# A gated cross-attention block with a mixture of experts: moving the low halves of expert weights to GpSimd and the shared chunk's first products into the last scores

## The chip, the cores and the metric

The kernel runs on one core of a Trainium2 chip. The metric is device microseconds of one execution. The core's engines are TensorE (PE, with its weight loads as PEld), VectorE (DVE), ScalarE (ACT), GpSimd (POOL) and SyncE (SP, which here only issues DMAs). Each engine has its own queue of instructions and works it off in order; semaphores order the engines against each other.

## What is computed

```python
def block(x, ctx, mask, g_xattn, g_ffn, ...):          # x: 16 x 128 x 256
    x = x + tanh(g_xattn) * cross_attention(layernorm(x), ctx, mask)   # 16 heads of 16
    h = layernorm(x)                                    # 2048 tokens of 256
    top2, idx = top_k(h @ w_router, 2)                  # 8 experts
    moe = sum over the 2 chosen e: softmax(top2)[e] * ((silu(h @ fc1[e][:, :256]) * (h @ fc1[e][:, 256:])) @ fc2[e])
    shared = (silu(h @ gate_w) * (h @ up_w)) @ down_w   # inner width 512
    return x + tanh(g_ffn) * (moe + shared)
```

## The kernel before, in words

The 2048 tokens are worked in G = 8 groups of 256 for the attention, and in 4 chunks of 512 for the shared feed-forward part. The attention of group g runs in a software pipeline over steps s: keys, queries, scores (once for the row maxima, once transposed for the exponentials), values, the second normalization, the router, and the places of the tokens in the experts' lists. All engines' orders are written out by hand, function by function.

**The way to the experts.** When the attention of the last group (g = 7) ends, four things have to be done before the first expert tile can start:

- The routing of the last units. `logits`, `choice` and `chosen` (DVE) make one-hot choices, `positions` (PE, lines 1527 to 1548) counts them, `places` (DVE, from line 1048) turns them into row numbers, `weights` (DVE, from line 1068) writes the weight and the destination into the rows and raises `w_ok`. Then `dispatch(g)` (POOL, lines 529 to 543) scatters the group's rows with four indirect DMAs into the DRAM tensor `dispatched`. `dispatch(7)` waits for `w_ok` of the last unit.
- `table` (DVE, lines 1186 to 1215) makes three things: `pads_ok`, on which SP issues eight DMAs of zero rows (line 451); `table_ok`, the row number of every tile; `words_ok`, the expert of every tile, which PE reads into registers (lines 1720 to 1723). SP loads the first tiles (line 473) when all scatters and pads have landed.
- The weights are split into a high half (ACT, `high_of_fc1` line 704, `high_of_fc2` line 778) and a low half, weight minus high half (`low_of_fc1`, line 1174, `low_of_fc2`, line 1180, both on DVE in the kernel before). There are E = 8 experts; one fc1 half is 128 x 1024 numbers, one fc2 half 128 x 512. PE waits for all 8 fc1 low halves ahead of the first `expert_h` (line 1771) and for all fc2 low halves ahead of the first `expert_y` (line 1797). GpSimd makes the low halves of the shared gate, up and down weights at line 589, after `f2lo_ok` has reached 8.
- The shared part of chunk 0 (`shared_0` line 1550, then `down_0` line 1582) and of chunk 1 (`shared_1(n)`, line 1567, n = 0 to 15, four to a block j of 128 hidden columns; then the loop at line 1730, in which `expert_x` transposes the first two tiles). ACT's `gate_silu` (line 787) and DVE's `times` (line 1168) take a block each from PSUM. `sum_and_add` (line 1158) adds the chunk's result.

From there 39 expert tiles follow each other on PE (lines 1810 to 1823). For each, GpSimd scatters the result (line 597); DVE's `expert_dst` (line 1269) writes the number of tile n into one of four places and waits until the scatter of tile n - 4, which used the place before, has landed. Chunks 2 and 3 of the shared part end the kernel.

PSUM banks of chunk 1: `BANKS_1` gives block j the banks (gate, up) by j % 2; the score tiles use banks 0 and 1, the transposed ones 2 and 3.

Of the kernel before, what the change touches and what calls it, by code (L numbers as in the profile page):

```python
# [7 lines left out]
ALU = mybir.AluOpType  # L8
ACT = mybir.ActivationFunctionType
F32 = mybir.dt.float32  # L10
# [43 lines left out]
def build_program(nc, x, ctx_t, mask, gates, wq, wk, wv, w_router, fc1, fc2, gate_w, up_w, down_w, out):  # L54
# [23 lines left out]
    with ExitStack() as es:  # L78
# [245 lines left out]

        BANKS_0 = (5, 6)
        EARLY = 4
        BANKS_1 = [(2, 3), (0, 1)]

        def live(g):

# [161 lines left out]
        def _(pool):  # L492
# [36 lines left out]
            def dispatch(g):  # L529
                u = g // 2 if g < 6 else g - 3  # L530
                if g == units[u][0]:
                    pool.wait_ge(slots_ok, u + 1)
                    pool.wait_ge(w_ok, u + 1)
                    pool.wait_ge(dup_ok[0], units[u][-1] + 1)
                    pool.wait_ge(dup_ok[1], units[u][-1] + 1)
                for m in range(4):
                    if (g, m) == (G - 4, 1):
                        power2(G - 1, 0)
                    if (g, m) == (G - 3, 0):
                        power2(G - 1, 1)  # L540
                    nc.gpsimd.indirect_dma_start(  # L541
                        xs, bass.IndirectOffsetOnAxis(slot_u[:, g, m:m + 1], 0), rows_of[g][:, m, :], None,
                        bounds_check=NULL_ROW + P - 1, oob_is_err=False).then_inc(scat[u == 1] if g else scat_first, 16)
# [27 lines left out]
            for s in range(2, G + 2):  # L571
# [6 lines left out]
                if live(s):  # L578
                    third(s, kst, k_rest, k_ok[1], k_pc, k_ok[2])
                    stack_k_high(s)  # L580
                    third(s, qst, q_rest, q_ok[1], q_pc, q_ok[2])

            dispatch(G - 4)
            dispatch(G - 3)
            dispatch(G - 2)
            dispatch(G - 1)

            def low_half(low, w, high):
# [16 lines left out]
                    low_half(xt_lo[:, :, tokens], xt_all[:, :, tokens], xt_hi[:, 2 * c - 4:2 * c - 2, :])  # L605


            for n, (low, w, high) in enumerate(((gate_lo, gate_s, gate_hi), (up_lo, up_s, up_hi),
                                                (down_lo, down_s, down_hi))):
                pool.wait_ge(gu_done, NJ)  # L610
                pool.wait_ge(f2lo_ok, E)
                if n == 2:
                    pool.wait_ge(down_done, 2 * CH)
                pool.wait_ge(high_ok, n + 1)
                low_half(low[:, :, :], w[:, :, :], high[:, :, :])
# [5 lines left out]
        def _(sa):  # L621
# [156 lines left out]
            def high_of_fc2(e):  # L778

                if e < EARLY:  # L780
                    sa.wait_ge(fc2_in, 16 * EARLY)
                else:
                    sa.wait_ge(fc2_late, 16 * (E - EARLY))
                nc.scalar.activation(fc2_hi[:, 2 * e:2 * e + 2, :], fc2_s[:, 2 * e:2 * e + 2, :],
                                     ACT.Copy).then_inc(f2hi_ok, 1)

            def gate_silu(c, j, bank):
                sa.wait_ge(gu_done, (c - 1) * NJ + j + 1)
                if c == 1 and j < 2:
                    sa.wait_ge(scat[1], ALL_1)  # L790
                else:
                    sa.wait_ge(hid_ok, (c - 1) * NJ + j - 1)
                nc.scalar.activation(sil_sh[:, j % 2], ps[:, bank, :], ACT.Silu).then_inc(sil_ok, 1)
# [36 lines left out]
            gate_silu(1, 1, BANKS_1[1][0])  # L830
            for e in range(6, E):
                high_of_fc1(e)
            for e in range(E):
                high_of_fc2(e)
            sa.wait_ge(scat_first, 64)
            sa.wait_ge(scat[0], ALL_0)
            sa.wait_ge(scat[1], ALL_1)
            sa.wait_ge(down_done, CH)
            high_half(gate_hi[:, :, :], gate_s[:, :, :])
            gate_silu(1, 2, BANKS_1[0][0])  # L840
            high_half(up_hi[:, :, :], up_s[:, :, :])
            gate_silu(1, 3, BANKS_1[1][0])
            high_half(down_hi[:, :, :], down_s[:, :, :])

            def rows_in_halves(t, d):
# [57 lines left out]
        def _(ve):  # L903
# [273 lines left out]
                nc.vector.tensor_tensor(fc1_lo[:, 2 * e:2 * e + 2, :], fc1_s[:, 2 * e:2 * e + 2, :],  # L1177
                                        fc1_hi[:, 2 * e:2 * e + 2, :].bitcast(F32), ALU.subtract).then_inc(flo_ok, 1)

            def low_of_fc2(e):  # L1180

                ve.wait_ge(f2hi_ok, e + 1)
                nc.vector.tensor_tensor(fc2_lo[:, 2 * e:2 * e + 2, :], fc2_s[:, 2 * e:2 * e + 2, :],  # L1183
                                        fc2_hi[:, 2 * e:2 * e + 2, :].bitcast(F32), ALU.subtract).then_inc(f2lo_ok, 1)

            def table():

                ve.wait_ge(pos_done, len(units))
# [48 lines left out]
            logits(g)  # L1237
            choice(g)
            chosen(g)
            places(g)  # L1240
            weights(g)
            table()
            relink()
            times(1, 0)
            times(1, 1)
            for e in range(3):
                low_of_fc1(e)
            sum_and_add(0, 0, sums_0)
            for e in range(3, 7):
                low_of_fc1(e)  # L1250
            times(1, 2)
            low_of_fc1(7)
            for e in range(3):
                low_of_fc2(e)
            times(1, 3)
            for e in range(3, E):
                low_of_fc2(e)

            def expert_rows(t, d):

# [102 lines left out]
        def _(pe):  # L1363
# [203 lines left out]
            def shared_1(n):  # L1567

                j, up, k = n // 4, n // 2 % 2, n % 2
                if n == 0:  # L1570
                    pe.wait_ge(xt_ok, 4)
                    pe.wait_ge(probs_ok[1][1], G)
                elif n == 4:
                    pe.wait_ge(max_ok[1][1], G)
                elif n % 4 == 0:
                    pe.wait_ge(hid_ok, j - 1)
                last = nc.tensor.matmul(ps[:, BANKS_1[j % 2][up], :], (gate_s, up_s)[up][:, k, P * j:P * j + P],
                                        xt_all[:, k, CH * P:2 * CH * P], start=k == 0, stop=k == 1)
                if n % 4 == 3:
                    last.then_inc(gu_done, 1)  # L1580
# [39 lines left out]
            for s in range(2, G + 2):  # L1620
                if live(s - 1):
                    queries(s - 1)
                if live(s - 2):
                    scores(s - 2, 1, 0)
                    if s == G + 1:
                        shared_0(6)
                    max_t(s - 2, 0)
                if live(s - 3):
                    values(s - 3, 1, 0)
                    values(s - 3, 1, 1)  # L1630
                if s == G + 1:
                    shared_0(7)
                if live(s - 4):
                    router(s - 4)
                if live(s - 2):
                    scores(s - 2, 1, 1)
                if live(s):
                    normed_t(s)
                    keys_main(s)
                if live(s - 3):  # L1640
                    values_t(s - 3, 1)
                if live(s - 2):
                    scores_t(s - 2, 0, 0)
                    if s == G:
                        shared_0(0)
                        shared_0(1)
                    if s == G + 1:
                        shared_0(8)
                if live(s):
                    values_main(s)  # L1650
                if live(s - 2):
                    max_t(s - 2, 1)
                if live(s):
                    for c in range(2):
                        keys_rest(s, c)
                        values_rest(s, c)
                if s == G:
                    shared_0(2)
                    shared_0(3)
                if s == G + 1:  # L1660
                    shared_0(9)
                    shared_0(10)
                if live(s - 2):
                    scores_t(s - 2, 0, 1)
                if live(s - 1):
                    scores(s - 1, 0, 0)
                if live(s - 4):
                    positions(s - 4)
                if live(s - 2):
                    values(s - 2, 0, 0)  # L1670
                    values(s - 2, 0, 1)
                    if s == G + 1:
                        shared_0(11)
                    scores_t(s - 2, 1, 0)
                if live(s - 1):
                    scores(s - 1, 0, 1)
                if s == G:
                    shared_0(4)
                if live(s - 2):
                    values_t(s - 2, 0)  # L1680
                if live(s - 3):
                    tokens_t(s - 3)
                if s == G:
                    shared_0(5)
                if live(s - 2):
                    scores_t(s - 2, 1, 1)

            g = G - 1
            values(g, 1, 0)
            router(g - 1)  # L1690
            values(g, 1, 1)
            values_t(g, 1)
            for n in range(12, 16):
                shared_0(n)
            positions(g - 1)
            tokens_t(g)
            shared_1(0)
            shared_1(1)
            router(g)
            for n in range(2, 5):  # L1700
                shared_1(n)
            positions(g)
            for n in range(5, 8):
                shared_1(n)
            for t in range(CH):
                down_0(t)
            for n in range(8, 16):
                shared_1(n)
# [175 lines left out]
```

## Time and profile before

| | |
|---|---|
| median of 3 runs | 333.09 us (332.68 to 334.06) |
| span of the profiled execution, first to last instruction | 329.2 us |
| the profiled execution's own time | not given apart; the runs' median lies 3.9 us above the span |
| PE, DVE, ACT, POOL busy | 304.6, 243.6, 169.2, 129.8 us |
| mean granted TensorE clock | 0.983 of full speed |
| first expert product | starts 190.84 us into the span |

Line numbers (L1177) are lines of the kernel. In a timeline a row gives the start, the duration, the engine, the line, the operation with output and inputs, how many instructions are merged (x4), and in brackets how long the engine was idle before and who ended that. In the chain of waits a row is one piece of the chain that ended last, with its start and its length.

### The profile page before, as it was taken

What the parts mean: (1) busy time and instruction counts of PE and PEld (TensorE: products, weight loads), DVE (VectorE), ACT (ScalarE), POOL (GpSimd) and SP (SyncE); (2) the same over time, 40 slices, a digit from 0 to 9 for tenths busy, and PEclk for the clock granted to TensorE, in tenths of its full rate; (3) what the DMA queues carried; (4) which work ended last, traced back from release to release, by engine and by line L of the source; (5) the groups of instructions that cost most, each with busy time, mean ns of one, the idle gap of its engine ahead of it and who ended that gap; (6) DMA issues with size and microseconds to landing.
All of it is one profiled execution on the core that took longest, in us unless ns stands there. A gap on an engine that the chain in (4) does not pass through costs nothing.

```text
span 329.2 us, 8082 instructions
## 1 busy us (share of the span) xinstructions
PE 304.6 (93%) x2505; PEld 244.5 (74%) x2505; DVE 243.6 (74%) x728; ACT 169.2 (51%) x322; POOL 129.8 (39%) x151
## 2 busy tenths in 40 slices
PE   7948889999989979998999989999999999999986
PEld 7627667787768755655465758889988898888875
DVE  4576597798999998687679976666666666633895
ACT  2444767777777744365495236444454444424131
POOL 5732143232465744506760085744333433331000
PEclk9998999999999999996999999999999999999999
DMA  7882776586666362166226112333333333103941
GB/s 232 255 217 80 227 197 207 161 263 193 189 186 177 123 178 84 50 201 250 98 98 164 44 34 83 106 94 108 94 103 98 97 85 111 64 16 133 416 153 64
DMA packets 34069, 47.18 MB, mean 143 GB/s; under 512 B 5519, under 2 KB 27667, under 8 KB 33522
## 3 DMA queue, kind: packets, MB, share of 16 engines
q1 hardware_dynamic: 28706, 34.61, 35.3%
q0 software_dynamic: 4320, 10.92, 9.9%
q10 hardware_dynamic: 1008, 1.18, 1.2%
q8 instruction: 22, 0.36, 0.5%
q14 instruction: 13, 0.11, 0.1%
HBM read 22.20 MB, written 12.62 MB: 106 GB/s over the span
## 4 chain that ended last, share of the span: by engine, by line
PE 41%; DVE 18%; issue 17%; POOL 8%; DMA 7%; SPq 5%; ACT 2%; POOLq 0%; DVEq 0%
PE ps L1744 27%; POOL dispatched L541 4%; DMA stacks<-work 4%; DVE x_all L1334 3%; DVE fc_lo L1177 3%; SPq L381 3%; PE ps L1790 3%; PE ps L1716 2%; PE ps L1562 2%; POOL rs L526 2%; PE ps L1437 1%; SPq L374 1%; DVE fc_lo L1183 1%; DMA stacks<-expert_rows 1%; PE ps L1407 1%
## 5 line engine op out<-in xcount | busy, mean ns | idle before, releaser
L597 POOL DMA_INDIRECT expert_rows<-v_s,slot_u x39 | 38.3, 982 | 58.6 <-ACT v_s L867 46.3
L963 DVE TENSOR_REDUCE mx<-ps 128x8 f32<-128x1024 f32 x32 | 39.1, 1223 | 13.0 <-PE ps L1437 12.7
L1284 DVE TENSOR_TENSOR act<-ps,sil 128x256 f32<-128x256 f32 x39 | 16.6, 425 | 29.9 <-ACT sil L860 29.8
L549 POOL TENSOR_TENSOR work<-work 128x512 bf16<-128x512 f32 x16 | 18.5, 1156 | 50.3 <-ACT work L646 50.2
L677 ACT ACTIVATE probs<-ps 128x1024 f32<-128x1024 f32 x32 | 32.7, 1022 | 9.4 <-PE ps L1470 9.4
L860 ACT ACTIVATE sil<-ps 128x256 f32<-128x256 f32 x39 | 15.0, 384 | 41.4 <-PE ps L1744 41.3
L1744 PE MATMUL ps<-fc_hi,xs_hi 128*128 x78 | 34.2, 439 | 1.4 <-DVE xs_lo L1265 1.4
L1744 PE MATMUL ps<-fc_hi,xs_lo 128*128 x78 | 30.7, 394 | 0.0
L1744 PE MATMUL ps<-fc_lo,xs_hi 128*128 x78 | 30.7, 394 | 0.0
L867 ACT ACTIVATE v_s<-ps,wt 128x256 f32<-128x256 f32 x39 | 18.5, 475 | 19.0 <-PE ps L1744 19.0
L1437 PE MATMUL ps<-stacks 96*128 96x128 bf16 x256 | 20.1, 222 | 7.0 <-DVE mx L963 3.3
L1437 PEld LDWEIGHTS ps<-stacks 96*128 96x128 bf16 x256 | 16.0, 100 | 10.3 <-DVE mx L963 4.8
L1744 PE MATMUL ps<-fc_hi,act_hi 128*128 x78 | 22.1, 283 | 0.2 <-DVE act_lo L1295 0.2
L1744 PE MATMUL ps<-fc_lo,act_hi 128*128 x78 | 22.0, 282 | 0.0
L1744 PE MATMUL ps<-fc_hi,act_lo 128*128 x78 | 21.9, 281 | 0.0
L1470 PEld LDWEIGHTS ps<-stacks 99*128 99x128 bf16 x256 | 15.8, 98 | 6.9 <-issue 5.4
L1470 PE MATMUL ps<-stacks 99*128 99x128 bf16 x256 | 19.7, 220 | 0.5 <-ACT probs L677 0.5
L1486 PE MATMUL ps<-probs,v_s 128*32 128x128 f32 x512 | 18.6, 281 | 1.1 <-DVE att L985 0.8
L1293 DVE CAST act_hi<-ps 128x256 fp32r<-128x256 f32 x39 | 16.5, 423 | 3.2 <-PE ps L1790 3.2
L541 POOL DMA_INDIRECT dispatched<-row_s,slot_u x16 | 16.0, 1000 | 7.4 <-issue 4.1
L1295 DVE TENSOR_TENSOR act_lo<-ps,act_hi 128x256 fp32r<-128x256 f32 x39 | 16.6, 424 | 1.3
L526 POOL TENSOR_TENSOR rs<-ve,mhalf 128x1 f32<-128x1 f32 x16 | 9.1, 566 | 21.4 <-DVE ve L996 21.4
(221 smaller groups left out, 828.4 us busy)
## 6 DMA issues: line engine op xcount, KB each, us to landing
stacks<-work SPq DMA_DIRECT2D x75, 128.0 KB, 3.1
xs_in<-dispatched SPq DMA_DIRECT2D x39, 129.0 KB, 2.0
fc_s<-in_fc SPq DMA_DIRECT2D x8, 512.0 KB, 5.2
stacks<-work POOLq DMA_DIRECT2D x18, 128.0 KB, 3.4
ctx_s<-in_ctx_t SPq DMA_DIRECT2D x8, 256.0 KB, 3.7
fc_s<-in_fc SPq DMA_DIRECT2D x8, 256.0 KB, 5.3
stacks<-expert_rows SPq DMA_DIRECT2D x2, 1024.0 KB, 5.8
probs<-expert_rows SPq DMA_DIRECT2D x2, 1024.0 KB, 9.9
```

The lines of the kernel that those rows point to most:

```text
L541: nc.gpsimd.indirect_dma_start(xs, bass.IndirectOffsetOnAxis(slot_u[:, g, m:m + 1], 0), rows_of[g][:, m, :], None, bounds_check=NULL_ROW + ...
L549: nc.gpsimd.tensor_tensor(out[:, 2, :], rest, out[:, 1, :], ALU.subtract).then_inc(ready, 1)
L597: nc.gpsimd.indirect_dma_start(ys, bass.IndirectOffsetOnAxis(dst_u[:, r:r + 1], 0), y_out[:, r, :], None, bounds_check=2 * T - 1, oob_is_e ...
L677: nc.scalar.activation(probs[:, 2 * j + h], ps_t, ACT.Exp, scale=HD ** -0.5).then_inc(probs_ok[j][h], 1)
L867: nc.scalar.activation(y_out[:, r, :], ps[:, 5 + r % 2, 0:D], ACT.Copy, scale=wt[:, r:r + 1]).then_inc(y_ok, 1)
L963: nc.vector.reduce_max(mx[:, j, 8 * h:8 * h + 8], ps_s, AX_X).then_inc(max_ok[j][h], 1)
L1284: nc.vector.tensor_tensor(act[:, par], ps[:, 2 + par, FI:2 * FI], sil[:, par], ALU.mult).then_inc(act_ok, 1)
L1295: nc.vector.tensor_tensor(act_lo[:, par], whole, act_hi[:, par].bitcast(F32), ALU.subtract).then_inc(actt_ok, 1)
L1437: last = nc.tensor.matmul(ps_s[:, n, :], q_st[at], k_st[at], start=True, stop=True)
L1470: last = nc.tensor.matmul(ps_t[:, n, :], k_st[at], q_st[at], start=True, stop=True)
L1486: last = nc.tensor.matmul(ps_o[row:row + VW, blk:blk + P], v_s[:, g % 2, j, VW * head:VW * head + VW], probs[:, 2 * j + h, n, :], start=Tr ...
L1744: ins = nc.tensor.matmul(out, a, b, start=first and n == 0, stop=last and n == 2)
```

## The change

The low halves of fc2 (8) and those of fc1's experts 0 and 1 move from DVE to GpSimd. The two fc1 ones stand between `dispatch(6)` and `dispatch(7)`, the eight fc2 ones behind `dispatch(7)` and ahead of the shared weights' low halves. On PE the first four `shared_1` calls move into the end of group 7's attention, `shared_1(4)` to `(7)` ahead of the last router, and `down_0(0)` ahead of the last `positions`. `BANKS_1` is swapped, and with it which wait stands at n = 0 and n = 4. On DVE one fc1 low half goes between `chosen(7)` and `places(7)`, the two first `times(1, j)` go around `weights(7)` and ahead of `table`, and the other low halves are put between the sums and products. On ACT `gate_silu(1, 2)` and `(1, 3)` go ahead of the wait for the scatters.

```diff
-        BANKS_1 = [(2, 3), (0, 1)]
+        BANKS_1 = [(0, 1), (2, 3)]
...
+            def low_of_fc1(e):
+                pool.wait_ge(fhi_ok, e + 1)
+                nc.gpsimd.tensor_tensor(fc1_lo[:, 2 * e:2 * e + 2, :], fc1_s[:, 2 * e:2 * e + 2, :],
+                                        fc1_hi[:, 2 * e:2 * e + 2, :].bitcast(F32), ALU.subtract).then_inc(flo_ok, 1)
+
+            def low_of_fc2(e):
+                pool.wait_ge(f2hi_ok, e + 1)
+                nc.gpsimd.tensor_tensor(fc2_lo[:, 2 * e:2 * e + 2, :], fc2_s[:, 2 * e:2 * e + 2, :],
+                                        fc2_hi[:, 2 * e:2 * e + 2, :].bitcast(F32), ALU.subtract).then_inc(f2lo_ok, 1)
...
             dispatch(G - 2)
+            low_of_fc1(0)
+            low_of_fc1(1)
             dispatch(G - 1)
...
+            for e in range(E):
+                low_of_fc2(e)
             for n, (low, w, high) in enumerate(((gate_lo, gate_s, gate_hi), (up_lo, up_s, up_hi),
...
             gate_silu(1, 1, BANKS_1[1][0])
             for e in range(6, E):
                 high_of_fc1(e)
-            for e in range(E):
+            for e in range(4):
                 high_of_fc2(e)
+            gate_silu(1, 2, BANKS_1[0][0])
+            for e in range(4, E):
+                high_of_fc2(e)
+            gate_silu(1, 3, BANKS_1[1][0])
             sa.wait_ge(scat_first, 64)
...
             chosen(g)
+            low_of_fc1(2)
             places(g)
+            times(1, 0)
             weights(g)
+            times(1, 1)
             table()
             relink()
-            times(1, 0)
-            times(1, 1)
-            for e in range(3):
-                low_of_fc1(e)
             sum_and_add(0, 0, sums_0)
-            for e in range(3, 7):
-                low_of_fc1(e)
+            low_of_fc1(3)
             times(1, 2)
+            low_of_fc1(4)
+            low_of_fc1(5)
+            times(1, 3)
+            low_of_fc1(6)
             low_of_fc1(7)
-            for e in range(3):
-                low_of_fc2(e)
-            times(1, 3)
-            for e in range(3, E):
-                low_of_fc2(e)
...
                 if s == G:
                     shared_0(5)
+                if s == G + 1:
+                    shared_1(0)
                 if live(s - 2):
                     scores_t(s - 2, 1, 1)
 
             g = G - 1
+            shared_1(1)
             values(g, 1, 0)
             router(g - 1)
+            shared_1(2)
             values(g, 1, 1)
+            shared_1(3)
             values_t(g, 1)
             for n in range(12, 16):
                 shared_0(n)
             positions(g - 1)
             tokens_t(g)
-            shared_1(0)
-            shared_1(1)
+            for n in range(4, 8):
+                shared_1(n)
             router(g)
-            for n in range(2, 5):
-                shared_1(n)
+            down_0(0)
             positions(g)
-            for n in range(5, 8):
-                shared_1(n)
-            for t in range(CH):
+            for t in range(1, CH):
                 down_0(t)
             for n in range(8, 16):
                 shared_1(n)
```

## Rows read from the trace of the kernel before

**Rows 1.** The chain that ended last, 136 to 200 us: start, length, what.

```profile
153.59 5.49 PE ps L1562 x8
...
160.18 1.72 PE ps L1577 x4
...
165.59 0.19 DVE slot L1054
...
167.36 0.18 DVE row L1082
...
168.02 0.16 DVE pad_i L1193
...
171.95 0.07 DVE eid_w L1215
...
173.35 3.40 DVE fc_lo L1177 x3
176.75 1.57 DVE x_all L1165 x4
...
187.00 3.01 DVE fc_lo L1183 x5
```

**Rows 2.** Windows: stretch, length, busy PE PEld DVE ACT POOL, clock, DMA share, GB/s.

```profile
148.00:149.00 1.00, 0.34 (x7) 0.16 (x3) 0.90 (x5) 0.78 (x2) 0.10 (x1) 1.00 0.92 236
...
151.00:152.00 1.00, 0.77 (x16) 0.32 (x8) 0.53 (x4) 0.17 (x1) 0.39 (x1) 0.50 1.05 422
```

**Rows 3.** Timeline of PE, 136 to 205 us.

```profile
168.07 7.07 PE L1588 MATMUL ps<-down_s,hid_a 128*128 128x256 f32 x32
...
181.84 5.34 PE L1736 MATMUL ps<-down_s,v_s 128*128 128x256 f32 x24
...
190.84 0.49 PE L1744 MATMUL ps<-fc_hi,xs_hi 128*128 x1 [1.40 <-DVE xs_lo L1265]
```

**Rows 4.** Timeline of POOL, 136 to 215 us.

```profile
162.44 0.98 POOL L541 DMA_INDIRECT dispatched<-row,slot_u  x1 [0.85 <-issue]
...
190.15 2.39 POOL L589 TENSOR_TENSOR gate_lo<-gate_s,gate_hi 128x1024 fp32r<-128x1024 f32 x1 [16.72 <-DVE fc_lo L1183]
```

**Rows 5.** Timeline of all engines, 120.5 to 122.5 us.

```profile
120.80 1.15 POOL L549 TENSOR_TENSOR work<-work 128x512 bf16<-128x512 f32 x1 [4.55 <-ACT work L646]
120.92 1.05 DVE L1085 TENSOR_SCALAR dest_f<-dest_f 128x8 f32<-128x8 f32 x1
```

**Rows 6.** Lines 1085, 1066 and 549: durations in ns, least, median, most.

```profile
L1085 DVE TENSOR_SCALAR dest_f<-dest_f x3: 172/1052/1056, 89.7 to 148.1; 128x8 f32<-128x8 f32 x3
...
L1066 DVE TENSOR_TENSOR cum<-cum,new x4: 167/168/1046, 83.3 to 160.4; 128x8 bf16<-128x8 bf16 x4
...
L549 POOL TENSOR_TENSOR work<-work x16: 1152/1156/1162, 13.8 to 120.8; 128x512 bf16<-128x512 f32 x16
```

**Rows 7.** Timelines of SP and ACT, 136 to 215 us.

```profile
171.30 4.42 SPq L451 DMA_DIRECT2D dispatched<-zrow  x8
179.21 34.44 SPq L473 DMA_DIRECT2D xs_in<-dispatched  x13
...
168.47 0.59 ACT L793 ACTIVATE sig<-ps 128x512 f32<-128x512 f32 x1
...
177.73 1.06 ACT L796 ACTIVATE gate_hi<-gate_s 128x1024 fp32r<-128x1024 f32 x1 [2.63 <-DMA dispatched<-row,slot_u]
```

**Rows 8.** The page, DMA issues: KB each, median us to landing.

```profile
xs_in<-dispatched SPq DMA_DIRECT2D x39, 129.0 KB, 2.0
```

**Rows 9.** Timelines of POOL and DVE in the first expert tiles.

```profile
198.73 0.99 POOL L597 DMA_INDIRECT expert_rows<-v_s,slot_u  x1 [1.49 <-ACT v_s L867]
...
202.56 0.14 DVE L1275 COPY wt<-xs_in 128x1 f32<-128x1 f32 x1
...
205.18 1.00 POOL L597 DMA_INDIRECT expert_rows<-v_s,slot_u  x1 [0.16 <-issue]
...
208.13 0.15 DVE L1275 COPY wt<-xs_in 128x1 f32<-128x1 f32 x1 [0.22 <-DMA expert_rows<-v_s,slot_u]
```

More of the change, by code:

```diff
@@ L839, in _ @@
             high_half(gate_hi[:, :, :], gate_s[:, :, :])
-            gate_silu(1, 2, BANKS_1[0][0])
             high_half(up_hi[:, :, :], up_s[:, :, :])
-            gate_silu(1, 3, BANKS_1[1][0])
             high_half(down_hi[:, :, :], down_s[:, :, :])
@@ L1178, in low_of_fc1 @@
                                         fc1_hi[:, 2 * e:2 * e + 2, :].bitcast(F32), ALU.subtract).then_inc(flo_ok, 1)
[L1180 to L1184, printed above, removed]
             def table():
@@ L1571, in shared_1 @@
                     pe.wait_ge(xt_ok, 4)
+                    pe.wait_ge(max_ok[1][1], G)
+                elif n == 4:
                     pe.wait_ge(probs_ok[1][1], G)
-                elif n == 4:
-                    pe.wait_ge(max_ok[1][1], G)
                 elif n % 4 == 0:
```

## The prediction

> **What bounds the kernel now.** I read the page first: no engine fills the span, and an average says little about one stage. So the chain of waits came next, cut to 136 to 200 us. From 165.6 us on it runs on DVE alone: places, weights and table until 172.0, then two products, all sixteen low halves and four sums until 190.0 [rows 1]. The reader is to see that the way to the experts is bound by DVE. The windows show a second loss: PE is busy only 0.34 of the microsecond at 148, and at 151 its granted clock is 0.50 (1.2 GHz) [rows 2]; eight records then take 5.49 us where four take 1.72 later (2.4 GHz) [rows 1]. PE's timeline has little room behind DVE: it waits only 1.40 us for the first expert product, at 190.84 [rows 3]. POOL's has 16.72 us of idleness up to 190.15, which the change fills [rows 4]. Last, I looked for what DVE and POOL do to each other when both compute, since the change makes them do so at length [rows 5, 6].
>
> **The change part by part.**
>
> *Scores' end (PE).* A shared call is two records at 0.43 us (1.72 / 4 [rows 1]), so 0.86. Four calls go into the holes from 147 to 153, 3.45 us of dense work; the one ahead of the last transposed scores delays the attention's end by some 0.6. I take it that the clock then stays at 2.4 GHz, since the 0.34 window is what they fill. Shared calls 12 to 15 of chunk 0 need 3.45 instead of 5.49 us. With the 0.95 that the pieces before them lose (half of the 1.9 us in which they run between 151 and 153.6), the half clock costs 3.0 now. places(6), which hangs on PE's end of those calls at 159.1, comes 1.6 earlier, and so does w_ok of group 6: at 160.0 instead of 161.6, where dispatch(6) now ends a wait of 0.85 [rows 4].
>
> *The last router.* It stood behind two shared calls and now behind four (+1.72), so it starts when it does now, near 161.8. The choices on DVE end at 164.5, and the fc1 low half behind them (3.40 / 3 = 1.13 [rows 1]) at 165.6, when places start now. That low half is free: its cover is PE, which puts down_0(0) (7.07 / 4 = 1.77 [rows 3]) ahead of positions. Without that cover it costs 1.1.
>
> *POOL between dispatch(6) and (7).* Dispatch(6) follows dispatch(5) at 161.9, four DMAs, and ends near 166.7. An fc1 low half has the gate's shape, 128x1024: 2.39 us [rows 4]. Two fill 166.7 to 171.5, and all four DMAs of dispatch(7) are queued behind them.
>
> *What these two do to DVE.* Places end at 166.4; times(1, 0) (0.65, half of the 1.33 between table's end and 173.35 [rows 1]; one operand in PSUM) ends at 167.05; then weights(7) begin, six small operations on SBUF. In the rows a small DVE operation on SBUF that meets a GpSimd tensor_tensor takes 1.05 us instead of 0.17 and ends 0.02 after GpSimd's [rows 5]; lines 1085 and 1066 show it three times, 1.046 to 1.056 us [rows 6]. So the first of weights(7) is held until 169.1, and the next, by the second low half, until 171.5. w_ok comes at 172.1 instead of 167.5. That is the largest term, 4.6 us, and nothing covers it. Behind it stand times(1, 1) (0.6) and table (167.54 to 172.02, 4.5), which ends at 177.1, and dispatch(7), which starts 0.85 after w_ok as dispatch(6) does now [rows 4], at 172.9, and ends at 177.9 instead of 173.43 (190.15 less 16.72).
>
> *SP's queue.* The pads leave 3.1 us after pads_ok at 168.2 [rows 1], at 171.30, and the first tile when they have landed, at 179.21 [rows 7]. Both slide by 5.1. Tiles 0 and 1 leave from 184.3 on, land 2.0 later [rows 8], and expert_x of tile 1 ends at 187.45. The last four products of chunk 1 (5.34 / 3 = 1.78 [rows 3]) end at 189.2: PE can start no expert earlier, whatever DVE does. ACT's three high halves, which wait for the scatters until 177.73 [rows 7], slide to 182.1 to 185.3, still ahead of the tiles.
>
> *DVE after table.* Sums (1.57 [rows 1]) end at 178.7; five fc1 low halves (1.13 each) and two products (1.25) remain, unhindered until 185.7 instead of 190.0. But POOL now makes eight fc2 halves from 177.9 on, 128x512 each: 1.16 us by line 549 [rows 6], 1.2 as half of 2.39; I take 1.2, the same operation. DVE's halves wait for the one running. No row shows GpSimd waiting for DVE; the bounds for that are nothing (line 549 keeps to 1152 to 1162 ns) and DVE's whole operation. I take the upper end, since the only wait of this kind that the rows have lasts for the whole operation. Then they alternate at 2.35 us a pair: 179.1 + 4 x 2.35 + 1.15 = 189.65. With the 0.83 from the last low half (190.01 [rows 1]) to the first product, that product is at 190.5, 0.35 earlier than now. With the lower end DVE ends at 187.45 and the tiles decide, 189.2.
>
> By the Trainium skill, SBUF — State Buffer, section "Who interferes with whom", a DVE instruction with two SBUF inputs and a GpSimd instruction that reads SBUF exclude each other, and the one that starts first blocks the other for its whole length. The trace agrees in one direction (1.05 us) and shows nothing of the other; by that rule the sum is the alternating one.
>
> *POOL behind it.* Its fc2 halves end at 193.25, early enough for the first expert_y, whose result is scattered at 198.73 now [rows 9]; the three shared halves end at 200.4 instead of 197.2. Scatter 0 leaves at 200.55. It lands some 2.7 later (scatter 2 of 205.18 releases tile 6's number after a wait of 0.22, at 208.1 [rows 9]), and tile 4's number wants it, now at 202.56 [rows 9], then at 202.2. DVE waits some 0.9; for PE the bounds are 0 and 0.9, since only DVE's slack in a tile lies between, and I take 0.35.
>
> **Sum.** -0.35 + 0.35 = 0. The span stays 329.2; the runs' median, 333.09, lies 3.9 above it, which I leave as it is: 333.1 us. This case's own range is 331.5 (lower end of the hold) to 334.6 (0.2 us more a pair for handing over, and the late scatter in full).
>
> **The rivals.**
>
> *No hold that matters.* GpSimd and DVE work freely beside each other. For it: only small operations were seen held. Against: [rows 6], to the whole length of GpSimd's. Then weights end at 168.1, table waits only for ACT's second silu (168.47 now [rows 7]) and slides by 2.0; the tiles allow 186.1, and DVE is done at 182.5: -4.7, 328.4 us.
>
> *One-sided hold.* POOL doesn't wait for DVE's halves: 189.2 as worked out, no late scatter, -1.6, 331.5 us.
>
> *Slower: PE starves ahead of chunk 1's down products.* The shared calls end at 177.1, when words_ok comes; reading eight numbers took SP 3.1 us [rows 1, 7], so five take some 2. PE stands still until 179.4, from 184.8 to 187.0 for tiles, and again for DVE. If that has the clock at 1.2 GHz when the experts start, a stretch like that of 151 costs 3.0: 336.1 us. For it: the 0.34 window [rows 2]. Against: the wait of 1.40 at 190.84, after which nothing slows [rows 3]. It decides from the point where the low clock outlasts 189.
>
> *The shared calls don't keep the clock up.* The half clock comes at 151 all the same, the last router is 2.9 late, and DVE meets both low halves already in places: 336.0 us.
>
> **How the numbers follow.** A measurement of this kernel tells 0.5%, 1.7 us, from no change. Chances: forecast 0.40, no hold 0.20, one-sided 0.15, starved 0.17, clock not kept 0.08. Faster takes the second and 0.07 of the third, which lies on the edge: 0.27. Slower takes the last two: 0.25. The same: 0.48. The range, 328.2 to 336.3, reaches to the outer cases, each a little widened.
>
> **What would show it.** Right: operations of weights(7) of one to two microseconds that end with GpSimd's low halves; w_ok near 172; fc1 halves on DVE or fc2 halves on GpSimd stretched to some 2.3; the first product at 189 to 191; a granted clock of 1.00 over 150 to 157. Wrong: weights(7) at 0.16 us an operation beside a running GpSimd low half, with a first product near 186; or windows at 0.50.

## The result, and the profile after

The changed kernel takes 344.47 us (median of 4 runs, 342.23 to 345.25) against 332.88 us (4 runs, 331.25 to 334.06): a ratio of 1.0318, 95% interval 1.0275 to 1.0362 (the two medians alone give 1.035). It is slower by 3.2%, outside the predicted range. The profiled execution took 345.24 us for a span of 343.5, 1.7 more; the profiled one of before, span 329.2, was thus a quick one of its kernel, at some 331 us.

The end of the attention came out as predicted. Where PE was busy 0.34 of a microsecond at 148 and the granted clock was 0.50 at 151 [rows 2], PE is now full and the clock 1.00, and the last four shared calls of chunk 0 (line 1569) take 3.44 us in the chain instead of 5.49 [rows 1]. The windows of the changed kernel show that, and what comes 30 us later (stretch, length, busy PE PEld DVE ACT POOL, clock, DMA share, GB/s):

```profile
151.00:152.00 1.00, 1.00 (x10) 0.48 (x6) 0.96 (x3) 0.57 (x1) 0.50 (x1) 1.00 0.97 256
...
184.00:186.00 2.00, 0.00 (x0) 0.00 (x0) 2.00 (x1) 0.83 (x1) 2.00 (x3) 0.68 1.16 185
186.00:192.00 6.00, 0.00 (x0) 0.00 (x0) 6.00 (x3) 2.11 (x3) 5.55 (x6) 0.50 0.41 106
192.00:198.00 6.00, 4.93 (x12) 3.95 (x13) 6.00 (x7) 0.00 (x0) 6.00 (x2) 0.50 0.01 3
```

PE does nothing from 184 to 192. From 186 to 192 DVE has three instructions and GpSimd six: DVE counts as busy, but it is held. DVE's timeline names the instructions:

```profile
165.84 0.17 DVE L1031 COPY lg<-ps 128x16 f32<-128x16 f32 x1 [1.85 <-PE ps L1529]
...
169.36 5.17 DVE L1078 CAST slot_u<-slot_f 128x4 uint32<-128x4 f32 x1
...
175.77 0.17 DVE L1098 COPY row<-dest_f 128x4 f32<-128x4 f32 x1
...
181.01 0.18 DVE L1224 TENSOR_REDUCE word_f<-eid_s 1x5 f32<-1x40 int32 x1
181.22 10.23 DVE L1225 CAST eid_w<-word_f 1x5 int32<-1x5 f32 x1
191.37 1.64 DVE L1181 SCALAR_TENSOR_TENSOR x_all<-ps,tg,x_all 128x256 f32<-128x256 f32 x4
192.94 1.20 DVE L1193 TENSOR_TENSOR fc_lo<-fc_s,fc_hi 128x1024 fp32r<-128x1024 f32 x1
...
194.68 6.63 DVE L1193 TENSOR_TENSOR fc_lo<-fc_s,fc_hi 128x1024 fp32r<-128x1024 f32 x2
```

A cast of five numbers takes 10.23 us, one of four columns 5.17; before, the first took 0.20 in the timeline and stood in the chain with 0.07 [rows 1]. Reading such a row means laying GpSimd's timeline beside it:

```profile
168.82 0.97 POOL L541 DMA_INDIRECT dispatched<-row,slot_u  x1 [0.30 <-issue]
169.81 4.69 POOL L585 TENSOR_TENSOR fc_lo<-fc_s,fc_hi 128x1024 fp32r<-128x1024 f32 x2
...
180.64 0.97 POOL L541 DMA_INDIRECT dispatched<-row,slot_u  x1 [0.31 <-issue]
181.62 9.80 POOL L590 TENSOR_TENSOR fc_lo<-fc_s,fc_hi 128x512 fp32r<-128x512 f32 x8
191.88 5.05 POOL L601 TENSOR_TENSOR gate_lo<-gate_s,gate_hi 128x1024 fp32r<-128x1024 f32 x1 [0.45 <-POOL fc_lo L590]
196.90 3.33 POOL L601 TENSOR_TENSOR up_lo<-up_s,up_hi 128x1024 fp32r<-128x1024 f32 x1
```

Both casts begin in the last part of an indirect DMA and end with GpSimd's low halves: with both of fc1's (169.81 + 4.69 = 174.50; the cast ends at 174.53), and with all eight of fc2's (191.42 against 191.45), not with the first of them. Later the engines take turns: `gate_lo` lasts 5.05 us and `up_lo` 3.33 instead of 2.39 [rows 4], and two low halves on DVE 6.63 instead of 2.3. PE shows what that costs:

```profile
193.07 8.05 PE L1745 MATMUL ps<-down_s,v_s 128*128 128x256 f32 x24 [10.76 <-DVE x_all L1181]
...
205.00 0.50 PE L1753 MATMUL ps<-fc_hi,xs_hi 128*128 x1 [0.66 <-DVE xs_lo L1272]
```

The first expert product starts at 205.00 instead of 190.84 [rows 3]. From there to the end the span has 138.5 us left, as before (329.2 - 190.84 = 138.4): the whole loss lies ahead of that product. Of the 14.3 us between the two spans a part belongs to the execution, not to the change: a granted clock of 0.50 at 122 to 126, ahead of all changed instructions (1.00 there before), had made this one 2.6 us late by 149. So executions are best compared from a common point, the copy of the last router's logits (`lg`, 162.95 before, 165.84 after), in three stretches:

| us | before | after | predicted |
|---|---|---|---|
| `lg` to w_ok (end of weights(7)) | 4.6 | 10.1 | 9.2 |
| w_ok to the words (end of `eid_w`) | 4.6 | 15.5 | 5.0 |
| words to the first product | 18.7 | 13.6 | 13.4 |
| `lg` to the first product | 27.9 | 39.2 | 27.6 |

With 0.1 from the last stretch to the end, 39.16 - 27.89 + 0.14 = 11.4 us of loss, against 11.6 between the medians.

### The profile page after: what moved, and what is told of

Same layout as the page of the kernel before. It is cut to its first block, busy times and chain, and to the rows that moved or that the text cites. A ratio compares the mean times of both kernels' runs of the same rounds, so it can differ in the third digit from the quotient of the medians.

```text
span 343.5 us, 8082 instructions
## 1 busy us (share of the span) xinstructions
PE 308.8 (90%) x2505; PEld 247.3 (72%) x2505; DVE 255.7 (74%) x718; ACT 169.3 (49%) x322; POOL 147.6 (43%) x161
## 4 chain that ended last, share of the span: by engine, by line
PE 50%; DVE 25%; issue 8%; DMA 7%; SPq 5%; ACT 3%; POOL 1%; DVEq 0%; POOLq 0%; ACTq 0%
PE ps L1753 26%; PE ps L1569 4%; DMA stacks<-work 3%; DVE fc_lo L1193 3%; SPq L381 3%; DVE x_all L1341 3%; DVE mx L979 3%; PE ps L1799 2%; PE ps L1414 2%; PE ps L1725 2%; PE ps L1493 2%; PE ps L1444 2%; PE ps L1477 2%; PE ps L1584 2%; DVE slot_u L1078 2%
## 5 line engine op out<-in xcount | busy, mean ns | idle before, releaser
L979 DVE TENSOR_REDUCE mx<-ps 128x8 f32<-128x1024 f32 x32 | 39.1, 1223 | 15.5 <-PE ps L1444 15.0
L867 ACT ACTIVATE xs_hi<-ps 128x256 fp32r<-128x256 f32 x39 | 14.8, 382 | 14.5 <-PE ps L1725 14.3
L1745 PE MATMUL ps<-down_s,v_s 128*128 128x256 f32 x32 | 9.9, 480 | 10.8 <-DVE x_all L1181 10.8
```

The lines of the kernel that those rows point to most:

```text
L979: nc.vector.reduce_max(mx[:, j, 8 * h:8 * h + 8], ps_s, AX_X).then_inc(max_ok[j][h], 1)
```

## The experiments

In each, the number to compare is the stretch from `lg` to the first product, beside the time.

**Fc2's low halves back on DVE**

```diff
-            for e in range(E):        # GpSimd
-                low_of_fc2(e)
+            for e in range(E):        # DVE, behind low_of_fc1(7)
+                low_of_fc2(e)
```

> All eight fc2 low halves are back on DVE, behind its last fc1 one; the two fc1 ones stay on GpSimd. Theory 'held for a whole run': a DVE cast that is caught by a GpSimd DMA waits until the whole row of GpSimd tensor_tensors behind it is over. Then the cast of the slots still takes some 5.2 us, the cast of the words 0.2 instead of 10.2; DVE gets 4.8 us of fc2 halves back and loses the 4.3 us for which GpSimd's gate and up halves held its fc1 ones. First expert product some 9 us earlier than in the changed kernel, 335 us. Rival 'order': the time went into the new order of PE and DVE and not into GpSimd: then this is slower than the changed kernel by the 4.8 us, 349 us.

337.53 us, ratio 1.017 (1.011 to 1.023); `lg` to the product 29.7 us. The words' cast takes 0.38 us, no low half is stretched, and the slots' cast takes 5.15 as in the changed kernel. The stretch is 9.5 us shorter than in the changed kernel, as expected; the median is 6.9 lower (344.47 - 337.53), 2.5 above the time expected. What fc2's low halves on GpSimd cost thus lies between 7 and 9.5 us; the difference is taken up below.

**Fc1's two low halves back on DVE**

```diff
-            low_of_fc1(0)             # GpSimd, between dispatch(6) and (7)
-            low_of_fc1(1)
+            low_of_fc1(0)             # DVE, behind the first sum
+            low_of_fc1(1)
```

> The two fc1 low halves are back on DVE, behind the first sums; the fc2 ones stay on GpSimd. Held for a whole run: the slots' cast takes 0.2 instead of 5.2 us, so dispatch(7) and table come 5 us earlier; if the words' cast is again caught by the last DMA of dispatch(7), it is held 10 us as before, and the time is 341 to 343 us; if it slips through ahead of it, the products of fc2 on GpSimd and fc1 on DVE only take turns, and it is 335 to 337. Rival 'order': 2.3 us slower than the changed kernel, 347.

342.49 us, ratio 1.0324 (1.0261 to 1.0386): the time is the first theory's, but the held operation is another one. DVE's timeline in this kernel, and then GpSimd's:

```profile
175.12 10.37 DVE L1219 TENSOR_SCALAR base_i<-base_f 1x39 int32<-1x39 f32 x1
...
185.61 2.36 DVE L1221 TENSOR_TENSOR eid_s<-eid_i,bits 1x40 int32<-1x40 int32 x1
188.00 0.18 DVE L1222 TENSOR_REDUCE word_f<-eid_s 1x5 f32<-1x40 int32 x1
188.22 2.02 DVE L1223 CAST eid_w<-word_f 1x5 int32<-1x5 f32 x1
```

```profile
174.63 0.97 POOL L541 DMA_INDIRECT dispatched<-row,slot_u  x1 [0.30 <-issue]
175.62 9.83 POOL L590 TENSOR_TENSOR fc_lo<-fc_s,fc_hi 128x512 fp32r<-128x512 f32 x8
185.57 2.34 POOL L599 TENSOR_TENSOR gate_lo<-gate_s,gate_hi 128x1024 fp32r<-128x1024 f32 x1
187.87 2.34 POOL L599 TENSOR_TENSOR up_lo<-up_s,up_hi 128x1024 fp32r<-128x1024 f32 x1
```

With w_ok 5 us earlier the run of eight starts earlier and catches `base_i` of the table, again from the last part of an indirect DMA, again for the whole run. Behind it `eid_s` and the words' cast are held for one GpSimd operation each, to the ends of `gate_lo` and `up_lo` (187.91 and 190.21); the reduction between them is not held at all. So DVE gets in between `gate_lo` and `up_lo`, although the second follows the first without a gap. Ahead of `up_lo` three waits for semaphores stand in the program, all long met, ahead of each fc2 low half one; whether that matters was not tried.

**All low halves on DVE, the changed orders kept**

> All low halves on DVE as in the kernel before, and everything else as in the changed kernel: the orders, banks and shared calls inside the last scores alone. Held for a whole run: no cast is held, clock stays at 2.4 GHz over 150 to 157, DVE saves the 1.1 us of the half that lies in its wait: 331 to 333 us, the same as before or a little faster. Rival 'order': 340 us or more.

334.97 us, ratio 1.0113 (1.0012 to 1.0214), four runs between 332.82 and 337.79; `lg` to the product 27.95, as before. The expected gain is missed: DVE has all its old work to do in this stretch and stays the bound. PE, whose work was moved ahead, is done early and stands 5.33 us; the first product then runs at half clock, first PE's row, then a window:

```profile
191.09 0.79 PE L1759 MATMUL ps<-fc_hi,xs_hi 128*128 x1 [5.33 <-DVE xs_lo L1278]
```

```profile
190.00:194.00 4.00, 2.91 (x7) 2.23 (x8) 2.61 (x9) 0.00 (x0) 3.60 (x2) 0.50 0.13 37
```

**The words written without a cast**

```diff
-                link(nc.vector.reduce_sum(word_f[:, :], ...))
-                nc.vector.tensor_copy(eid_w[:, :], word_f[:, :]).then_inc(words_ok, 1)
+                nc.vector.reduce_sum(eid_w[:, :], ...).then_inc(words_ok, 1)
```

> The changed kernel, but the words of the tiles' experts are written as whole numbers by the sum itself, without the cast behind it. Held for a whole run, and casts alone: nothing waits at table's end, though GpSimd's eight halves run as before; words come 10 us earlier. DVE's five fc1 halves, with two inputs on SBUF, then take turns with GpSimd's: first product some 8 us earlier, 336 us. If two-input operations are held for a whole run as well, the first fc1 half takes the cast's place and waits 8 us or more, and the time stays at 343 to 345 us.

344.09 us, ratio 1.0354 (1.0289 to 1.0418): the second figure. The words are ready at 182.35 and the sums follow at once, unheld, but the first low half behind them is held instead, from 1.1 us into GpSimd's run to its end, with its own 1.1 us behind that (DVE, then GpSimd):

```profile
183.88 9.82 DVE L1193 TENSOR_TENSOR fc_lo<-fc_s,fc_hi 128x1024 fp32r<-128x1024 f32 x1
```

```profile
182.78 9.83 POOL L590 TENSOR_TENSOR fc_lo<-fc_s,fc_hi 128x512 fp32r<-128x512 f32 x8
```

So it takes neither the cast nor the indirect DMA ahead of it: GpSimd's eight operations follow each other without a gap, and DVE, waiting, gets in behind the last one only.

**GpSimd waits for the words ahead of its run**

```diff
+            pool.wait_ge(words_ok, 1)
             for e in range(E):
                 low_of_fc2(e)
```

> The changed kernel with one wait more: GpSimd's first fc2 half waits for the words. Held for a whole run: the cast at table's end waits only for the last DMA of dispatch(7), at most 0.5 us instead of 10.2; GpSimd starts its eight halves less than 1 us later than in the changed kernel. If DVE's fc1 halves take turns with them, the first product is some 8 us earlier and the time 336 us; if those are held for the whole run too, 343 us. Rival 'port time': what counts is the sum of the time that both need the port, whoever comes first; then nothing changes, 344 us.

334.56 us (10 runs), ratio 1.0046 (1.0014 to 1.0077); `lg` to the product 28.0. The words' cast takes 0.39 us. Here the engines take turns from the start: the eight GpSimd halves need 14.93 us, DVE's four last ones 3.9 a pair. The first low half on DVE arrived at 183.36, within 0.1 us of the end of GpSimd's first operation (182.13 + 1.27), and was not held, although GpSimd's second operation had begun by then; that one took 2.36 us instead.

**A wait between GpSimd's low halves of fc2**

```diff
             for e in range(E):
+                if e:
+                    pool.wait_ge(f2lo_ok, e)
                 low_of_fc2(e)
```

> The changed kernel, in which each fc2 half on GpSimd waits for the end of the one before it, so that they no longer follow back to back; the same operations in the same place. Held for a whole run, because no gap lies between: the words' cast gets in at the first gap and takes 1.5 us at most instead of 10.2; first product some 8 us earlier, 336 us, and slower by 0.1 to 0.3 us for each wait. Rival 'held by the kind of operation': a cast waits as long as GpSimd has such work at hand, gap or not: 10 us and 344 us or more.

335.10 us (10 runs), ratio 1.007 (1.0035 to 1.0106); `lg` to the product 29.5 instead of 39.2. Work, order and engines are those of the changed kernel; only GpSimd now lets each half finish before it issues the next. DVE, then GpSimd:

```profile
179.46 1.73 DVE L1227 CAST eid_w<-word_f 1x5 int32<-1x5 f32 x1
```

```profile
179.87 15.37 POOL L590 TENSOR_TENSOR fc_lo<-fc_s,fc_hi 128x512 fp32r<-128x512 f32 x8
```

The cast ends with the first half (which takes 1.29 us, 179.87 + 1.29 = 181.16; the cast ends at 181.19). This run shows the cause: without the waits GpSimd's halves run on and DVE is kept out, with them 9.4 us between the medians come back (9.6 in the stretch).

**A single wait, ahead of the fifth of the eight**

```diff
             for e in range(E):
+                if e == 4:
+                    pool.wait_ge(f2lo_ok, 4)
                 low_of_fc2(e)
```

> The changed kernel with a single wait for the end of the one before, ahead of the fifth of GpSimd's eight low halves of fc2. If a held operation gets in at the first such wait, the words' cast takes the last part of the indirect DMA and four low halves, 5.2 to 5.4 us instead of 10.23, and the sums start 5 us earlier; DVE's next low half, which then meets the second four, is held by them in turn, to about the end of the eighth. The time is 340 to 343. If the hold has to do with the run's whole length, or with nothing but the operation itself, the cast takes 10 us again and the time is 344.

340.94 us (one run); `lg` to the product 34.2. The dose is right: the cast takes the indirect DMA's end and four halves. But the second four do not hold the next low half as a run; from there on the engines take turns, with no further wait in the program (DVE, then GpSimd):

```profile
181.81 5.38 DVE L1227 CAST eid_w<-word_f 1x5 int32<-1x5 f32 x1
...
188.67 1.20 DVE L1195 TENSOR_TENSOR fc_lo<-fc_s,fc_hi 128x1024 fp32r<-128x1024 f32 x1
...
190.40 3.89 DVE L1195 TENSOR_TENSOR fc_lo<-fc_s,fc_hi 128x1024 fp32r<-128x1024 f32 x2
```

```profile
182.21 13.21 POOL L590 TENSOR_TENSOR fc_lo<-fc_s,fc_hi 128x512 fp32r<-128x512 f32 x8
```

**A wait between fc1's two as well**

```diff
-            low_of_fc1(0)
+            pool.wait_ge(fhi_ok, 1)
+            nc.gpsimd.tensor_tensor(fc1_lo[:, 0:2, :], ...).then_inc(f2lo_ok, 1)
+            pool.wait_ge(f2lo_ok, 1)
             low_of_fc1(1)
```

(on top of the waits in fc2; the counts in the other waits follow.)

> The changed kernel with a wait for the end of the one before between all of GpSimd's low halves, the two of fc1 as well. If a held DVE operation gets in wherever GpSimd stands still for a semaphore, the cast of the slots is held for one low half, 2.8 us (from 5.18), w_ok comes 2.4 us earlier, the first expert product some 2 us earlier than where only fc2's were spaced, and the time is 333 us, 332 to 334, a ratio near 0.998. If what holds that cast is the indirect DMA or the cast's own form, it still takes 5.2 us and the time is 335.

335.44 us (9 runs, 333.06 to 337.61), ratio 1.0079 (1.0052 to 1.0105). The mechanism is confirmed at this second place, DVE first:

```profile
166.70 2.78 DVE L1083 CAST slot_u<-slot_f 128x4 uint32<-128x4 f32 x1
169.40 0.68 DVE L1192 TENSOR_TENSOR v_s<-ps,sig 128x512 f32<-128x512 f32 x1
170.00 1.92 DVE L1095 TENSOR_SCALAR den<-ex 128x2 f32<-128x2 f32 x1
```

```profile
167.06 2.38 POOL L597 TENSOR_TENSOR fc_lo<-fc_s,fc_hi 128x1024 fp32r<-128x1024 f32 x1
169.52 2.37 POOL L585 TENSOR_TENSOR fc_lo<-fc_s,fc_hi 128x1024 fp32r<-128x1024 f32 x1
```

The time is a miss. The cast gives back 2.4, but the next small operation on SBUF, `den`, meets the second half for 1.92 (0.15 in the changed kernel), so `lg` to the product falls by only 0.6, to 28.9, which the medians (335.10 and 335.44, ratios 1.007 and 1.0079) can't tell apart.

**More low halves in DVE's own waits**

In the orders of the changed kernel, but with all sixteen on DVE: fc1's first three ahead of `attended(7, 1)`, `logits(7)` and `places(7)`, where DVE waits for PE, and their high halves earlier on ACT.

> The orders of the changed kernel, all low halves on DVE, with fc1's 0, 1 and 2 placed where DVE waited for PE (ahead of the last attended rows, ahead of the last logits, ahead of the last places), and their high halves earlier on ACT, in its wait for the last values. Three halves of 1.13 us each are off DVE's way to the experts instead of one: 2.3 us less than the orders alone: 329 to 331 us, faster than both kernels. If instead the late table and tiles bound the start, no gain over the orders alone.

333.27 us (10 runs), ratio 0.9991 (0.9952 to 1.0031), a miss: `lg` to the product falls to 25.7, but the rest of the span grows by 1.8 (from 138.4 to 140.2): PE again stands 2.40 us ahead of the product and then needs 0.63 us for some products instead of 0.40.

**Fc2's last four on GpSimd, behind DVE's last low half**

```diff
-            for e in range(E):        # DVE
+            for e in range(4):
                 low_of_fc2(e)
...
+            pool.wait_ge(f2lo_ok, 4)  # GpSimd
+            for e in range(4, E):
+                low_of_fc2(e)
```

(on top of the kernel above; `down_lo` goes behind the first scatter.)

> The kernel with low halves in DVE's waits, and the last four low halves of fc2 on GpSimd, behind DVE's last one, with the down weight's low half behind the first scatter. If only meeting DVE's operations on SBUF makes GpSimd's low halves dear, they run at 1.25 us each, DVE's low halves end 2.4 us earlier, the first expert product comes 2.0 to 2.4 us earlier than with all sixteen on DVE, and the time is 331.5 us, a ratio of 0.994. If they still hold DVE's small operations of the first tiles, or the scatters get late, nothing is gained: 333 to 334 us.

331.14 us (12 runs), ratio 0.9939 (0.9906 to 0.9971): as expected, and faster than both kernels, than the one before by 0.6%. `lg` to the product is 23.3 us. DVE ends its low halves at 188.36, GpSimd begins there, at its own speed, and PE stands no longer (DVE, GpSimd, PE):

```profile
185.87 2.49 DVE L1204 TENSOR_TENSOR fc_lo<-fc_s,fc_hi 128x512 fp32r<-128x512 f32 x4
...
202.47 0.15 DVE L1297 COPY wt<-xs_in 128x1 f32<-128x1 f32 x1 [1.46 <-DMA expert_rows<-v_s,slot_u]
```

```profile
188.45 5.00 POOL L590 TENSOR_TENSOR fc_lo<-fc_s,fc_hi 128x512 fp32r<-128x512 f32 x4 [11.63 <-DVE fc_lo L1204]
```

```profile
189.19 0.50 PE L1768 MATMUL ps<-fc_hi,xs_hi 128*128 x1 [0.28 <-DVE xs_lo L1287]
```

Of the 4.6 us (27.9 - 23.3) the rest of the span takes back 1.7 (140.1 instead of 138.4), although the clock is 1.00 here: scatters are late, and DVE waits 1.46 us for one that it did not wait for before (202.56 in [rows 9]). PE waits 0.96 us for DVE there; where the other 0.7 goes was not traced. So the bill foreseen for a late scatter comes due in part here, where GpSimd works between the product and the first scatter.

## Why the prediction was wrong

- **The end of the scores** was right: full windows, a clock of 1.00 over 150 to 157, 3.44 instead of 5.49 us. Of the four profiles of the experiments with a clock of 1.00 from 118 to 147, two have `lg` at 163.1, near the 162.95 of before; the other two, whose clock was 0.94 instead of 0.98 over the first 80 us, have it at 164.05 and 164.70. So the last router starts about when it did, as said.
- **What the two fc1 halves do to DVE** was right as a mechanism and in size: 4.6 us forecast, 5.2 held. It caught one operation for both halves where the prediction had two held for one half each, and an earlier one: the slots' cast in places(7), not the first of weights(7). So times(1, 0) and weights(7), 1.4 us, came behind the hold, and w_ok 0.9 later than worked out. That small difference already showed the failing step.
- **The step that failed** is in the part on DVE after table: "DVE's halves wait for the one running", with table ending at 177.1 and the run of eight starting at 177.9. The wait of DVE was priced at one GpSimd operation, 1.2 us, and for table, ahead of the run, at nothing. The runs showed that DVE can be kept out for all eight, 9.8 us; the table's last operation arrives 0.4 us before the run, in the indirect DMA's last part, which holds it over into the run, and takes 10.23 us. The stretch from w_ok to the words took 15.5 us instead of 5.0. The experiment with a wait between the halves shows it: 9.4 us come back. Without that cast the next operation with two inputs in SBUF is held in its place, for 9.82 us.
- **What follows the words** came out in its number, 13.6 us against 13.4, by luck: with the words late the composition was another (two shared low halves took the turns, not eight of fc2, and DVE's sums came late with them). The price of a turn was right: where GpSimd waits for the words, its low halves beside DVE's begin 2.2 us apart, 2.35 forecast a pair. The scatter that was to be late by 0.35 was not: GpSimd's first one, at 212.91, waits 5.95 us for its data, as the tiles had become later than GpSimd's halves.
- **Both bounds lay on one side.** The prediction bounded how long GpSimd waits for DVE, and took for the hold of DVE the length of one GpSimd operation. The rows it rested on are three holds of 1.05 us beside a 1.15 us operation [rows 5, 6], and none has a run of low halves in it. In two of them (89.73 and 120.92) another GpSimd operation does follow without a gap, an `rs` of 128x1 (the row below, from the kernel before), and DVE gets in at the end of the first all the same. So the rows spoke for a hold of one operation; that they did not bound a longer run was the thing to see. With the whole run as the upper bound, 10 us more, a slower kernel would have had a mechanism and a price. The rival without any hold falls with the held casts, the one-sided one with GpSimd's eight low halves, which take 14.93 us beside DVE's.

```profile
121.91 0.55 POOL L526 TENSOR_TENSOR rs<-ve,mhalf 128x1 f32<-128x1 f32 x1
```

- **By the Trainium skill**, SBUF — State Buffer, section "Who interferes with whom", the one that starts first blocks the other for the whole instruction. The runs agree that the later one waits. They differ on how long: up to eight instructions (10.37 us, where one takes 1.25), so here the measurement decides. Held in the runs were casts, tensor_scalars and operations with two inputs in SBUF (low halves, `eid_s`); the reductions, and the sums and products with an input in PSUM, were not.
- **The rival that PE starves ahead of chunk 1's down products** named the place and the clock rightly (10.76 us, 0.50 from 186 to 198), and with all low halves on DVE a wait of 5.33 us and the low clock behind it show by themselves, at the first expert product, where the rest of the span grows by 2.0 us. In the changed kernel it is a result of DVE's wait.

For most kernels the medians agree with this account: the loss by the two stretches of the trace, `lg` to the product and product to end, is 11.4 us for the changed kernel (11.6 measured), 9.5 without fc1's halves on GpSimd (9.7), 11.1 without the cast (11.3). With waits between the halves of fc2 it is 2.7 (1.5), with one wait 6.5 (8.0, a single run). For fc2's back on DVE it is 2.2 (4.7 measured): that kernel's profiled execution had `lg` at 167.23, with a clock of 0.91 over the first 80 us (0.98 before), so the rest lies ahead of that stretch, and why its four runs all took as long is open.

## What to carry to other kernels

Before elementwise work is moved from DVE to GpSimd, list the small casts and scalar operations on SBUF that DVE must do while it runs, and take as the upper bound of each wait not one GpSimd operation but everything queued behind it without a wait. Start GpSimd's work when DVE's own on SBUF is done (331.14 us here, 333.27 with all of it on DVE), or let GpSimd wait for each operation's end (335.10 instead of 344.47, but no faster than the kernel before). While both need SBUF, the moved work is not parallel: fc2's eight halves take DVE 4.9 us, GpSimd 9.8 us when it keeps DVE out, and 15 us in turns.

## What was not expected of the hardware

- A waiting DVE operation got in only behind a whole gapless run of eight GpSimd operations: 10.23 us (a cast), 10.37 (a tensor_scalar), 9.82 (two inputs in SBUF), each over a run of 9.8. A wait for a semaphore between two of them lets it in: 1.73.
- Once DVE has got in between, the two take turns, even where GpSimd's program has no wait (8.2 us for the last four in the kernel with a single one). What makes a run keep DVE out is open: the gap alone does not decide it. DVE got in without one behind the 1.15 us operation at 120.80, between `gate_lo` and `up_lo` with fc1's halves on DVE, and in the changed kernel at 192.94, where its low half took 1.20 us although `gate_lo` had begun 1.06 us earlier.
- The last part of an indirect DMA on GpSimd holds a cast or a tensor_scalar by up to 0.5 us (in the changed kernel a cast at 166.80 took 0.43 us instead of 0.17, to the DMA's end at 167.23), and hands it on to the low half that follows it, as with the casts of 10.23 and 5.17 us and the tensor_scalar of 10.37.
